# A four-layer transformer block on one core: feed-forward products of 256 columns, normalisation on ScalarE, and a planner that runs past the end of a chunk

## The reference

```python
x = x + L0_xcond(ln(x), ctx, ctx, tau, fside)      # attention, 16 heads of 16, over 1601 context rows
x = x + L0_ffn(ln(x))                              # 8 experts, the best one a token
x = x + L1_xcond(ctx, ln(x), lenS2, pt)            # one head, a window of the context, tanh
x = x + L1_ffn(ln(x))                              # routing to 64 slots, top 8, a GRU and attention of slots

# L0_xcond: scores = q.k * tau + delta; softmax(scores / 4) @ v; @ Wo.T + bo
# L0_ffn:
logits = x @ router_w.T + router_b
probs  = softmax(logits); weights = max(probs); top1 = argmax(probs)
y_all  = einsum('bsd,eod->bseo', x, expert_w) + expert_b
out    = y_all[top1] * weights
# L1_ffn: h = gelu(x @ w1 + c); route = (h @ w2 + b2) / (|tau| + 0.1); alpha = softmax of the top 8
#         slot_input = alpha.T @ x / sum(alpha); ... ; out = (alpha @ slot_values) @ wo + bo
```

## Time and profile before

| | |
|---|---|
| median of 3 runs | 1205.0 us (1202.1 to 1208.08) |
| profiled execution | 1201.54 us, its span 1199.9 us |
| granted TensorE clock, mean | 0.916 of full speed |
| busy: TensorE, weight loads, VectorE, ScalarE, POOL | 1021.9, 411.0, 809.4, 562.3, 44.1 us |
| start, up to the first product with V | 151.9 us |
| chunk 2, first job to the next chunk's | 239 us |
| tail, the last chunk's jobs | about 131 us |
| L1125, maxima on VectorE | 1102 reductions, 568 ns each |
| L616, exps on ScalarE | 832, 597 ns each |
| L880, the experts' products | 256 records of 128x512, 612 ns each |
| L1254, the multiply-adds | 128, 483 ns each |

### The profile page before, as it was taken

The page is one execution under the profiler, slowest core; times in us unless marked ns, Lnnn a source line. Parts: engine busy times, 40 slices in busy tenths (PEclk is TensorE's granted clock), DMA queues, the critical chain, the costliest instruction groups (busy, mean ns, idle before and its releaser), DMA issues.

```text
span 1199.9 us, 13638 instructions
## 1 busy us (share of the span) xinstructions
PE 1021.9 (85%) x4812; PEld 411.0 (34%) x4812; DVE 809.4 (67%) x1820; ACT 562.3 (47%) x1019; POOL 44.1 (4%) x54
## 2 busy tenths in 40 slices
PE   6446999999988998988899989888999898696656
PEld 3322233232333333433433334333333343243424
DVE  4446978787767777777677777776777677644232
ACT  4121066667644545666445556664455466301210
POOL 3110000000000000000000000000000000100000
PEclk9876599999989999999899999998999899978665
DMA  8996000000100000001000000010000000100512
GB/s 248 146 112 220 1 1 14 15 1 14 33 1 14 1 14 1 14 1 49 1 14 1 14 1 14 1 49 1 14 1 14 1 15 1 49 0 1 146 49 70
DMA packets 44238, 40.65 MB, mean 34 GB/s; under 512 B 10109, under 2 KB 42334, under 8 KB 43914
## 3 DMA queue, kind: packets, MB, share of 16 engines
q1 hardware_dynamic: 41594, 38.17, 13.6%
q10 hardware_dynamic: 2496, 1.35, 0.8%
q0 software_dynamic: 80, 0.26, 0.2%
HBM read 29.52 MB, written 10.59 MB: 33 GB/s over the span
## 4 chain that ended last, share of the span: by engine, by line
issue 46%; PE 26%; DVE 11%; DMA 6%; SPq 5%; ACT 2%; DVEq 2%; POOL 2%; POOLq 0%; ACTq 0%
DVE mx L1125 8%; PE ps_o L814 7%; PE ps_e L977 7%; PE ps_m L735 6%; DMA k_parts<-alphaT 2%; SPq L395 2%; DMA k_stack<-q_stack 2%; DMA xres<-in_x 1%; SPq L443 1%; PE ps_m L1040 1%; ACT probs L616 1%; PE ps_m L926 1%; SPq L419 1%; PE ps_m L929 1%; DMA x<-xres 1%
## 5 line engine op out<-in xcount | busy, mean ns | idle before, releaser
L1125 DVE TENSOR_REDUCE mx<-ps_m 128x1 f32<-128x401 f32 x1102 | 578.0, 568 | 203.7 <-PE ps_m L735 196.2
L616 ACT ACTIVATE probs<-ps_e 128x512 f32<-128x512 f32 (+1 forms) x832 | 472.6, 597 | 405.6 <-PE ps_e L977 404.8
L735 PE MATMUL ps_m<-k_stack,q_stack 99*128 99x401 bf16 x1102 | 356.7, 353 | 40.8 <-DVE mx L1125 40.0
L977 PE MATMUL ps_e<-q_stack,k_stack 101*128 101x512 bf16 (+1 forms) x832 | 326.2, 392 | 8.3 <-ACT probs L616 6.2
L814 PE MATMUL ps_o<-probs,v_heads 128*32 128x512 f32 (+1 forms) x1664 | 226.9, 618 | 0.0
L977 PEld LDWEIGHTS ps_e<-q_stack,k_stack 101*128 101x128 bf16 (+1 forms) x832 | 82.6, 99 | 302.1 <-ACT probs L616 207.5
L735 PEld LDWEIGHTS ps_m<-k_stack,q_stack 99*128 99x128 bf16 x1102 | 109.9, 100 | 175.9 <-DVE mx L1125 124.8
L880 PE MATMUL ps_m<-expert_w,xnT 128*128 128x512 f32 x256 | 130.8, 612 | 16.2 <-DVE xb L1254 16.2
L1254 DVE SCALAR_TENSOR_TENSOR xb<-ps_m,hot,xb 128x256 f32<-128x256 f32 x112 | 54.1, 483 | 18.3 <-PE ps_m L880 9.2
L880 PEld LDWEIGHTS ps_m<-expert_w,xnT 128*128 128x128 f32 x256 | 47.7, 196 | 48.3 <-DVE xb L1254 24.7
L814 PEld LDWEIGHTS ps_o<-probs,v_heads 128*32 128x32 f32 (+1 forms) x1664 | 33.0, 108 | 64.7 <-issue 56.1
(11 more groups left out here) (215 smaller groups left out, 617.3 us busy)
## 6 DMA issues: line engine op xcount, KB each, us to landing
q_stack<-q_parts SPq DMA_DIRECT2D x114, 64.0 KB, 2.2
k_stack<-k_parts SPq DMA_DIRECT2D x18, 256.0 KB, 14.0
q_parts<-attn_chunk SPq DMA_DIRECT2D x6, 384.0 KB, 5.8
expert_w<-in_expert_wT SPq DMA_DIRECT2D x2, 1024.0 KB, 6.0
xres<-in_x SPq DMA_DIRECT2D x4, 512.0 KB, 3.8
x<-xres SPq DMA_DIRECT2D x4, 512.0 KB, 3.2
probs<-x SPq DMA_DIRECT2D x1, 2048.0 KB, 9.7
out<-probs SPq DMA_DIRECT2D x4, 512.0 KB, 2.9
```

The lines of the kernel that those rows point to most:

```text
L616: act.activation(probs[0:n, k % 2, h, :], ps_e[h % 2][0:n, :], ACT.Exp).then_inc(s["exp_done"], 1)
L735: pe.matmul(ps_m[:, (UNITS * n1 + u) % RING, 0:SPLIT], qst[0:MAX_ROW, g, h, P * t:P * t + P], kst[0:MAX_ROW, HG * g + h, QUARTER_START[q]: ...
L977: pe.matmul(ps_e[h % 2][0:n, :], kst[0:ROWS, HG * g + h, P * st:P * st + n], qst[0:ROWS, g, h, :], start=True, stop=True).then_inc(s["qk_r ...
L1125: dve.tensor_reduce(mx[:, q, col:col + 1], ps_m[:, (UNITS * n1 + u) % RING, 0:SPLIT], AX.X, ALU.max)\
```

## The change

1. **Products.** Each expert product of 512 columns becomes two of 256, so an e has four products, one to a quarter from `AT` on, in place of two at +0 and +2. `rows_by` (y0, y1, score0, score1) also gets one product to a quarter; these jobs now hold their bank 6 quarters in place of 3, and VectorE takes them at +4 in place of +2.
2. **Normalisation on ScalarE.** VectorE's `normal` goes from the jobs (it stays in the start). POOL gets `shift()` after each `rsqrt`: three operations on 128x4 that give `off` = -mean * rstd. ScalarE writes `xn` with four activations (Identity, scale `rstd`, bias `off`), two in each of the quarters t - 3 and t - 2, where t is the quarter of t1a, t2a or t3a.
3. **Statistics by tile.** `spread_stats` takes one tile to a quarter. The second norm's statistics are taken tile by tile, each after its last e (+6).
4. **Order.** gateT follows e1 (before: e3), gb0 and gb1 follow e2 (before: e15).
5. **Past the end.** `places()` repeats the fixed M and O for the next chunk, and what is left of a chunk's jobs runs at its quarters in the next chunk (`old`), ahead of the new chunk's jobs of the same quarter. After the last chunk it is run at once.

The quarters that `places()` gives, as worked out from `JOBS` of both:

| | ota | y0 | y1 | t1a | router | e0 | e1 | gateT | e2 | gb0 | e3 | e4 | e5 | e10 | e11 | e13 | e14 | e15 |
|---|---|---|---|---|---|---|---|---|---|---|---|---|---|---|---|---|---|---|
| before | 10 | 15 | 17 | 28 | 33 | 38 | 42 | 55 | 48 | 112 | 52 | 58 | 64 | 84 | 88 | 98 | 102 | 106 |
| after | 9 | 14 | 18 | 34 | 39 | 43 | 49 | 53 | 55 | 61 | 65 | 69 | 73 | 93 | 99 | 107 | 113 | 117 |

| | t2a | score0 | score1 | aTa | z0 | z1 | t3a | h | logits | slots | alphaT |
|---|---|---|---|---|---|---|---|---|---|---|---|
| before | 125 | 130 | 132 | 145 | 150 | 158 | 178 | 183 | 189 | 203 | 207 |
| after | 130 | 135 | 139 | 152 | 157 | 166 | 187 | 192 | 198 | 210 | 216 |

```diff
-JOBS = [("ota", None, 10, 3), ("otb", "ota", 2, 3), ("y0", "otb", 3, 3), ("y1", "y0", 2, 3), ("t1a", "y1", 11, 3),
-        ("t1b", "t1a", 2, 3), ("router", "t1b", 3, 2), ("e0", "router", 5, 6)]
-JOBS += [(f"e{i}", f"e{i - 1}", 4, 6) for i in range(1, 4)] + [("gateT", "e3", 3, 3), ("e4", "gateT", 1, 6)]
-JOBS += [(f"e{i}", f"e{i - 1}", 4, 6) for i in range(5, NE)]
-JOBS += [("gb0", f"e{NE - 1}", 4, 4), ("gb1", "gb0", 2, 4), ("t2a", "gb1", 11, 3), ("t2b", "t2a", 2, 3),
-         ("score0", "t2b", 3, 3), ("score1", "score0", 2, 3), ("aTa", "score1", 13, 3), ("aTb", "aTa", 2, 3),
-         ("z0", "aTb", 3, 9), ("z1", "z0", 8, 9), ("t3a", "z1", 20, 3), ("t3b", "t3a", 2, 3), ("h", "t3b", 3, 5),
-         ("logits", "h", 6, 2), ("slots", "logits", 14, 6), ("alphaT", "slots", 4, 3)]
+JOBS = [("ota", None, 9, 3), ("otb", "ota", 2, 3), ("y0", "otb", 3, 6), ("y1", "y0", 4, 6), ("t1a", "y1", 16, 3),
+        ("t1b", "t1a", 2, 3), ("router", "t1b", 3, 2), ("e0", "router", 4, 6), ("e1", "e0", 4, 6), ("gateT", "e1", 4, 3),
+        ("e2", "gateT", 1, 6), ("gb0", "e2", 4, 4), ("gb1", "gb0", 2, 4), ("e3", "gb1", 2, 6)]
+JOBS += [(f"e{i}", f"e{i - 1}", 4, 6) for i in range(4, NE)]
+JOBS += [("t2a", f"e{NE - 1}", 13, 3), ("t2b", "t2a", 2, 3),
+         ("score0", "t2b", 3, 6), ("score1", "score0", 4, 6), ("aTa", "score1", 13, 3), ("aTb", "aTa", 2, 3),
+         ("z0", "aTb", 3, 9), ("z1", "z0", 8, 9), ("t3a", "z1", 21, 3), ("t3b", "t3a", 2, 3), ("h", "t3b", 3, 5),
+         ("logits", "h", 6, 2), ("slots", "logits", 12, 6), ("alphaT", "slots", 4, 3)]
 def places():
     fixed = sorted([(q, q + 3) for q in O_AT] + [(q, q + 2) for q in M_AT])
+    fixed += [(HG * SLOTS + q, HG * SLOTS + end) for q, end in fixed]
...
 # POOL, after each rsqrt of the jobs
+            def shift():
+                pool.tensor_tensor(mean_2[:], mv[:, :, 0], neg_half[:], ALU.mult)
+                pool.drain()
+                pool.tensor_tensor(mean_2[:], mean_2[:], rstd[:], ALU.mult)
+                pool.drain()
+                pool.tensor_tensor(off[:], mean_2[:], mean_2[:], ALU.add).then_inc(s["off_ready"], 1)
...
 # ScalarE; called as normal(xa, AT["t1a"] - 3, 3 * c + 1), (xb, AT["t2a"] - 3, ...), (xres, AT["t3a"] - 3, ...)
+            def normal(src, at, n):
+                for t in range(TT):
+                    yield at + t // 2
+                    if t == 0:
+                        act.wait_ge(s["off_ready"], n)
+                    last = act.activation(xn[:, t, 0:D], src[:, t, :], ACT.Identity, bias=off[:, t:t + 1],
+                                          scale=rstd[:, t:t + 1])
+                last.then_inc(s["xn_ready"], 1)
...
 # each engine's chunk(c, work)
-                work = begin(behind(c - 1)) if c else None
+                old, work = work, begin(behind(c - 1)) if c else None
...
+                        go_on(old, HG * (SLOTS + k) + h)
                         go_on(work, HG * k + h)
...
-                go_on(work, NEVER - 1)
+                return work
...
 # TensorE
                 for i, t in enumerate(tiles):
-                    if i:
-                        yield AT[name] + i
                     for k in range(KT):
+                        yield AT[name] + KT * i + k
...
-                    for k in range(KT):
-                        yield AT[name] + 2 * k
-                        mm = pe.matmul(bank(name, c), xnT[:, k, P * t:P * t + P], expert_w[:, k, CT * j:CT * j + CT],
-                                       start=(k == 0), stop=(k == KT - 1))
+                    for n in range(2):
+                        for k in range(KT):
+                            yield AT[name] + KT * n + k
+                            mm = pe.matmul(bank(name, c)[:, D * n:D * n + D], xnT[:, k, P * t:P * t + P],
+                                           expert_w[:, k, CT * j + D * n:CT * j + D * n + D],
+                                           start=(k == 0), stop=(k == KT - 1))
                     filled(mm, name, c)
-                    if i == 3:
+                    if i == 1:
                         yield AT["gateT"]
...
 # VectorE
-                yield from spread_stats(xa, AT["y1"] + 3)
-                yield AT["t1a"] - 4
-                normal(xa, NC + 3 * c + 1)
+                yield from spread_stats(xa, AT["y1"] + 5)
...
                     taken(last, f"e{i}", c)
+                    if i == 2:
+                        yield AT["gb0"] + 3
+                        dve.drain()
+                        wait_filled(dve, "gb0", c)
+                        dve.tensor_tensor(xb[:, 0, :], xb[:, 0, :], bank("gb0", c)[:, 0:D], ALU.add)
+                        taken(dve.tensor_tensor(xa[:, 1, :], xa[:, 1, :], bank("gb0", c)[:, D:2 * D], ALU.add), "gb0", c)
+                        yield AT["gb1"] + 3
+                        take_sum(xa[:, 2:4, :], xa[:, 2:4, :], "gb1", c)
+                    if j == 3:
+                        yield AT[f"e{i}"] + 6
+                        dve.drain()
+                        dve.bn_stats(bst[:, t, :], xb[:, t, :])
```

More of the change, by code:

```diff
@@ L129, in job_numbers @@
         for q in range(HG * SLOTS):
+            if c >= 2:
+                order += [(name, c - 2) for name in AT if AT[name] == HG * SLOTS + q]
             if c:
@@ L135, in job_numbers @@
                 order.append(("o", NG * c + O_AT.index(q) - 1))
-        if c:
-            order += [(name, c - 1) for name in AT if AT[name] >= HG * SLOTS]
+    order += [(name, NC - 2) for name in AT if AT[name] >= HG * SLOTS]
     order.append(("o", NG * NC - 1))
@@ L254, in build @@
         rstd = sb("rstd", [P, TT])
+        mean_2 = sb("mean_2", [P, TT])
+        off = sb("off", [P, TT])
         neg_half = sb("neg_half", [P, TT])
@@ L555, in behind @@
                     rsqrt(NC + 3 * c + i)
+                    shift()
             for c in range(NC):
@@ L633, in behind @@
                 take_xnT(1, "otb", c, attT)
+                yield from normal(xa, AT["t1a"] - 3, 3 * c + 1)
                 yield AT["t1a"] + 2
@@ L643, in behind @@
                 taken(act.copy(gateT[:], bank("gateT", c)[0:TT * NX, 0:P]), "gateT", c)
+                yield from normal(xb, AT["t2a"] - 3, 3 * c + 2)
                 yield AT["t2a"] + 2
@@ L665, in behind @@
                                          bank(f"z{i}", c), ACT.Tanh), f"z{i}", c)
+                yield from normal(xres, AT["t3a"] - 3, 3 * c + 3)
                 yield AT["t3a"] + 2
@@ L680, in behind, with chunk @@
                 taken(act.copy(alphaT[0:NS, c * CT:c * CT + CT], bank("alphaT", c)[0:NS, :]), "alphaT", c)
-            def chunk(c):
-                work = begin(behind(c - 1)) if c else None
+            def chunk(c, work):
+                old, work = work, begin(behind(c - 1)) if c else None
                 for k in range(SLOTS):
@@ L690, in chunk @@
                         exp(c, k, h)
+                        go_on(old, HG * (SLOTS + k) + h)
                         go_on(work, HG * k + h)
-                go_on(work, NEVER - 1)
+                return work
+            work_left = None
             for c in range(NC):
-                chunk(c)
+                work_left = chunk(c, work_left)
+            go_on(work_left, NEVER - 1)
             take_o(NC, -1)
@@ L888, in behind @@
                                             ident[:]), "gateT", c)
-                for i in range(2):
-                    name = f"gb{i}"
-                    yield AT[name]
-                    wait_taken(pe, "gateT", c)
-                    bank_free(pe, name, c)
-                    for t in range(2):
-                        yield AT[name] + t
-                        mm = pe.matmul(bank(name, c)[:, D * t:D * t + D], gateT[:], eb[:, 2 * i + t, :], start=True, stop=True)
-                    filled(mm, name, c)
+                    for m in range(2 if i == 2 else 0):
+                        name = f"gb{m}"
+                        yield AT[name]
+                        wait_taken(pe, "gateT", c)
+                        bank_free(pe, name, c)
+                        for t in range(2):
+                            yield AT[name] + t
+                            mm = pe.matmul(bank(name, c)[:, D * t:D * t + D], gateT[:], eb[:, 2 * m + t, :],
+                                           start=True, stop=True)
+                        filled(mm, name, c)
                 yield AT["t2a"]
```

37 lines of the change are left out of this document (16 added, 21 removed).

## The result

The changed kernel takes 1248.5 us (median; 1247.4 to 1249.3), the kernel before beside it 1206.5: ratio 1.036, interval 1.033 to 1.038. It is slower by 42 us, where 1201 was forecast and 1216 was the upper end of the range. The profiled execution took 1249.26 us, its span 1247.5.

What follows compares the result with a forecast made beforehand. TensorE was taken to set the pace. From the profiled 1201.54 us, gains of 11.1 (chunks) and 2.5 (clock) less losses of 3.4, 1.0, 4.4 and 0.4 gave 1197.1; with 3.5 to the median, about 1201 us, range 1185 to 1216.

Steps and rivals of the forecast that it cites:

- Products: Feed-forward products in e slots: four of 256 columns gain 0.5 us a chunk, bounds -1.1 to +2.3; slots 4.4 to 4.6 us.
- Bank waits: TensorE waiting for job banks: six waits of 7.9 us a chunk, a loss of 2.4; bounds +2.8 to -4.2.
- Normalisations: Three norms a chunk, moved from VectorE to ScalarE: gains of 3.3, 2.0 and 0.7 us, 6.0 together.
- End before ScalarE asks: At each norm, POOL's three added operations, 0.88 us in all, finish in time, with three to four quarters between.
- Rival B: Exps stand behind ScalarE's normalisations waiting for POOL: 6 us a chunk, 13 over three, 1214 us; chance 0.22.
- Boundary: Slots and alphaT running into the next chunk: 1.7 us lost at each of two boundaries, 3.4; bounds 0 and 3 each.
- Tail: After the last chunk: norms 1.5 us longer each, 4.4 for three; leftover jobs 1.0 lost; feed-forward end 0.4 lost.
- The extra low clock: Chunks 1 and 3, one low-clock stretch each costing 5.1 us together: half, 2.5, counted as gained.
- maxima under 6 us: Sign of being right: in a chunk, maximum products wait under 6 us for VectorE in place of 10.
- no low clock 30 us into the chunk: Sign of being right: the low clock about 30 us into a chunk is gone.
- exps that wait behind POOL: Sign of being wrong: ScalarE's exps are held up waiting for POOL; no size given.
- a middle chunk: Sign of being wrong: a middle chunk takes under 231 or over 241 us.

Runs made afterwards that it cites:

- e2: In this text a job, one expert's products; as a run, the changed kernel with each chunk's jobs ended at the chunk's own end, 1249.8 us.
- e9: The changed kernel with never-read filler products ahead of only the row of three close bank waits in a chunk; 1236.3 us.
- e1: The changed kernel with 3 to 7 never-read filler products in TensorE's queue ahead of each of six waits of a chunk; 1222.7 us.
- e4: The changed kernel with the normalisations on VectorE again, statistics still one tile to a quarter, no shift on POOL; 1227.7 us.
- e14: The kernel of run e1 (waits filled) with the normalisations on VectorE again; 1204.1 us, ratio 1.000 to the kernel before.
- e3: The changed kernel with gateT, gb0 and gb1 put back in their old order; 1229.3 us.
- e7: The kernel before with never-read filler products ahead of four of its bank waits; 1203.8 us, ratio 0.9995.

## Why the prediction was wrong, step by step

- **Products** (+0.5 a chunk): right as far as the slot goes (4.57, inside 4.4 to 4.6). Alone on the kernel before they gave 8.5 us, in the changed kernel they cost 7 to 8; neither was in the sum, and neither is explained.
- **Bank waits** (7.9 a chunk): the waits were sized well, 6.6 (5.2 and 1.4 in chunk 2; e3 had none). **This is the first step that failed**: I priced a wait at its own length, though I had read low clock behind stalls in the earlier trace rows and charged it only where it already stood. The low clock behind e1, e2, gb0 and the others is the larger part, 12 us for the row of three alone (e9), 26 with the rest (e1).
- **Normalisations** (+6.0 a chunk): **the second step that failed.** Slots 5 to 7 take 10.71 us (3.70, 3.50, 3.51), the excess of 4.3 is 0.5, and in chunk 2 no low clock follows. But I gave that gain to ScalarE, and it isn't ScalarE's: with the norm on VectorE again (e4) the same slots take 3.70, 3.51 and 3.51, and slot 8, where the norm now stands, 4.05 in place of 4.85. There VectorE doesn't wait for POOL. What frees these slots is the norm's later place and the spread statistics. What ScalarE costs instead was mis-sized: 1.7 a chunk estimated, 3.4 more than on VectorE measured in waits at full clock, and the clock on top. "End before ScalarE asks" failed at all three norms: POOL's chain from var_e to off takes 2.2 us, and ScalarE waited for its end 0.61, 0.60 and 0.85 us in chunk 2, 6.7 us in the three chunks; an exp stands behind it each time. Rival B named this mechanism and its place. Its 13 us would only have eaten what the forecast gave the norms (18 gained in the chunks, 4.4 lost in the tail), while against VectorE the move costs 19 to 22; B took over the same gain, and left the clock out too.
- **Boundary** (1.7 each): slots 0 and 1 take 15.4 us in place of 6.7, slots 50 and 51 save 1.9 (measured like these from QK product to QK product), so 6.8 at chunks 2 and 3. alpha was the wait I named; its 1.79 us are what I took; 4.6 more are clock (e1).
- **Tail**: the norms are 1.5 us longer each, as forecast (from var_e to the normalised input 4.31 us against 2.77 in the earlier trace rows), 4.6 in all. The jobs left after the last chunk cost about 4, not 1.0 (e4's tail is 169.0 us with VectorE's norms, 165.1 before): slots waits 2.39 for alpha there. This part of the account is loose: e14 has the same tail as e4, and it took 173.4 us.
- **The extra low clock** (-2.5): wrong in sign. It was treated as a leftover that may go; the low time in the chunks rose from 29 to 96 us.
- **Slips in the sums**: 7.9 less 5.6 is 2.3 and not 2.4, and B with the bank waits at their bound is 1220 and not 1218. Neither changes the case.

Of the signs that I gave, maxima under 6 us (5.6), no low clock 30 us into the chunk, e slots, bank waits over 6 and the tail's norms all came true. So did two of the signs of being wrong: exps that wait behind POOL, and a middle chunk of 253 us, outside its bounds. The waits for banks and for alpha came out near the sizes that I gave them, and the sum still missed by 47 us, by two things: a clock that follows waits, and a gain that was put to the wrong part of the change. The clock alone doesn't close it: with the waits filled (e1) the kernel is still at 1222.7, above my range, with 54 us of low clock left in its chunks.

The Trainium skill, "TensorE: Matmul & The Clock Gate", section "A second HAM failure mode: psum-queue depth-cycling", tells of another kernel in which frequent small pauses of TensorE between groups of products make its clock swing between the two levels. The traces agree in kind (pauses of 0.9 to 1.8 us, then 1.2 GHz); I hadn't weighed it, and by it the new waits at the same six quarters speak against the change. The price comes from the runs.

## What to carry to other kernels

Price a stall of TensorE twice: its length, and the clock that may follow it. Which stalls it follows, these runs don't settle: nearly the same waits cost little of it in another order (e3), and none in the kernel before (e7). Test it with products that nobody reads: if the time falls, it was the clock. Where an order is planned with fixed distances, look for users that stand exactly at the distance at which the bank comes free; one quarter more was worth 16 us in the kernel before and 36 in the changed one. When a change has several parts, put each back alone before a gain is given to one of them: the norm's place paid, its engine did not. And count the engine in between (here POOL's power of 1.02 us) into the distance between the statistics and whoever uses them.
